# One-hot matrices of two edge stages written by GpSimd, one 128x128 comparison behind each gather, in place of VectorE

## The reference, cut to what matters

```
k_e = k[src] + e ; v_e = v[src] + e            # e = edge_attr @ We
alpha = einsum('ehd,ehd->eh', q[dst], k_e) / sqrt(16)
... softmax over the edges of a destination, then
out = segment_sum(attn * v_e, dst)
```

```
gates = softmax(gate_in @ W_gate + b_gate)      # 3 gates for each edge
out = gates[:,0]*x_src + gates[:,1]*x_dst + gates[:,2]*x_edge
return segment_sum(out, col)
```

## Time and profile before

| | us |
|---|---|
| median of 3 runs | 7088.67 (7060.04 to 7090.18) |
| span of the profiled execution | 7080.9 |
| keys-and-values stage, the gathers' stretch | 1444.0 |
| gate stage, the gathers' stretch | 1430.0 |

### The profile page before, as it was taken

The page is one execution under the profiler, slowest core; times in us unless marked ns, Lnnn a source line. Parts: engine busy times, 40 slices in busy tenths (PEclk is TensorE's granted clock), DMA queues, the critical chain, the costliest instruction groups (busy, mean ns, idle before and its releaser), DMA issues.

```text
span 7080.9 us, 98147 instructions
## 1 busy us (share of the span) xinstructions
PE 4162.5 (59%) x25513; PEld 3308.9 (47%) x25514; DVE 2977.6 (42%) x8318; ACT 1295.5 (18%) x3253; POOL 2894.8 (41%) x2784
## 2 busy tenths in 40 slices
PE   1112000599898455555563664798899666666664
PEld 1001000366565455555553563465565666556654
DVE  3438201411313344444446677212312555555556
ACT  0001000000100211111111664200200322322222
POOL 6778777000000265555553565000000255555555
PEclk6555555799899777777776996899999755655555
DMA  9713000366463455555552451464364222222222
GB/s 361 267 61 135 6 0 0 103 198 192 141 195 118 111 160 158 154 150 156 155 162 89 125 148 30 137 197 138 131 196 145 64 78 78 78 78 79 79 78 69
DMA packets 447985, 885.48 MB, mean 125 GB/s; under 512 B 91722, under 2 KB 278572, under 8 KB 441502
## 3 DMA queue, kind: packets, MB, share of 16 engines
q1 hardware_dynamic: 333406, 608.36, 27.1%
q0 software_dynamic: 106912, 224.30, 11.9%
q10 hardware_dynamic: 7584, 51.91, 2.0%
HBM read 728.93 MB, written 155.35 MB: 125 GB/s over the span
## 4 chain that ended last, share of the span: by engine, by line
PE 33%; DVE 20%; issue 19%; another core or an unknown queue 15%; DVEq 6%; DMA 2%; ACT 2%; ACTq 1%; SPq 0%; POOL 0%; POOLq 0%
PE ps L836 23%; DVE work L1603 3%; PE ps L992 2%; DVE work L624 2%; PE ps L415 1%; DVE work L368 1%; DMA hw<-d_keys 1%; DVE work L1202 1%; DVEq L342 1%; PE ps L1184 1%; DVE hw L438 1%; PE ps L843 1%; PE ps L1182 1%; DMA work<-attr_dram 1%
## 5 line engine op out<-in xcount | busy, mean ns | idle before, releaser
L361 POOL DMA_INDIRECT work<-tab_kv,src_col x832 | 814.1, 978 | 1758.7 <-DMA tab_kv<-hw 1142.1
L361 POOL DMA_INDIRECT work<-tab_gate,src_col x832 | 795.5, 956 | 1795.5 <-DMA tab_gate<-logits 1183.3
L484 POOL DMA_INDIRECT d_adj<-logits,address x782 | 848.1, 1085 | 276.6 <-issue 238.8
L836 PE MATMUL ps<-hw 128*128 128x384 bf16 x5096 | 863.4, 330 | 50.4 <-DVE hw L815 37.1
L836 PE MATMUL ps<-hw,work 128*128 128x384 bf16 x5096 | 845.1, 326 | 0.0
L415 PE MATMUL ps<-work 128*128 128x136 f32 (+1 forms) x3328 | 655.0, 360 | 131.6 <-DVE acc L438 86.4
L836 PEld LDWEIGHTS ps<-hw 128*128 128x128 bf16 x5096 | 502.1, 99 | 383.1 <-issue 53.7
L415 PEld LDWEIGHTS ps<-work 128*128 128x128 f32 x3328 | 599.8, 265 | 165.4 <-issue 165.4
L875 DVE TENSOR_TENSOR work<-work,ps 128x128 f32 (+1 forms) x208 | 59.9, 288 | 1410.0 <-ACT work L867 1409.2
L836 PEld LDWEIGHTS ps<-hw,work 128*128 128x128 bf16 x5096 | 498.8, 98 | 317.7
L1168 PE MATMUL ps<-ident,work 128*128 128x128 f32 x832 | 177.1, 350 | 656.8 <-ACT work L1158 285.2
(11 more groups left out here) (389 smaller groups left out, 6581.4 us busy)
## 6 DMA issues: line engine op xcount, KB each, us to landing
hw<-d_adj SPq DMA_DIRECT2D x104, 800.0 KB, 4.3
work<-d_adj SPq DMA_DIRECT2D x104, 800.0 KB, 4.4
d_adj<-acc SPq DMA_DIRECT2D x52, 1568.0 KB
hw<-d_adj SPq DMA_DIRECT2D x104, 768.0 KB, 4.2
work<-d_adj SPq DMA_DIRECT2D x104, 768.0 KB, 4.3
work<-attr_dram SPq DMA_DIRECT2D x832, 64.0 KB
d_value<-work SPq DMA_DIRECT2D x208, 256.0 KB
work<-d_value SPq DMA_DIRECT2D x208, 256.0 KB, 2.7
```

The source lines that it names most:

```text
L361: pool.indirect_dma_start(rows[:, r * U + u, 0:width], None, table, bass.IndirectOffsetOnAxis(sources[:, at:at + 1], 0)).then_inc(rows_in[ ...
L484: pool.indirect_dma_start(d_adj, bass.IndirectOffsetOnAxis(address[:, tile:tile + 1], 0), counts[:, tile:tile + 1], None).then_inc(adj_out ...
L836: last = nc.tensor.matmul(at, adj_half[2 * s + hf][:, k, :], xs[:, b, :], start=b == 0, stop=b == BLOCKS - 1)
```

## The change: where the one-hot matrices are written

Behind each gather GpSimd now writes the one-hot matrix of the same step itself: a comparison of 128x128 with the step's column of `rel_col` as the operand for each partition. Only the last comparison of a part adds to `hot_ready`. Before the first comparison of a part, and behind the part's first gather, GpSimd waits that the place of the matrices is free: on `att_turned` of part n - 4 in the keys-and-values stage, on `win_done` of part n - 4 in the gate stage. VectorE's two `step_hot` stages go; the one in the stage of the attention sums, which lies between the two, stays.

```diff
-        def gathers(pool, k, table, width, sources, free):
+        def gathers(pool, k, table, width, sources, free, hot_free):
             for n in range(GATHER_TURNS[k] * PARTS):
...
                 for u in range(U):
                     at = n * U + u
                     pool.indirect_dma_start(rows[:, r * U + u, 0:width], None, table,
                                             bass.IndirectOffsetOnAxis(sources[:, at:at + 1], 0)).then_inc(rows_in[r], 16)
+                    if u == 0 and n >= PARTS:
+                        hot_free(n - PARTS)
+                    ins = pool.tensor_scalar(hot[:, r * U + u, :], iota[:], rel_col[:, at:at + 1], None, ALU.is_equal)
+                ins.then_inc(sem("hot_ready"), 1)
...
-            gathers(pool, ATT_PASS, tab_kv, KV, src_col, lambda n: pool.wait_ge(sem("kv_done"), n + 1))
+            gathers(pool, ATT_PASS, tab_kv, KV, src_col, lambda n: pool.wait_ge(sem("kv_done"), n + 1),
+                    lambda n: pool.wait_ge(sem("att_turned"), n + 1))
...
-            edge_loop(dve, [(0, step_hot()), (2, scores)])
+            edge_loop(dve, [(2, scores)])
...
-            gathers(pool, GATE_PASS, tab_gate, GATE_ROW, src_col, lambda n: pool.wait_ge(sem("gate_msg"), n + 1))
+            gathers(pool, GATE_PASS, tab_gate, GATE_ROW, src_col, lambda n: pool.wait_ge(sem("gate_msg"), n + 1),
+                    lambda n: pool.wait_ge(sem("win_done"), gate_sums.done0 + U * (n + 1)))
...
-            edge_loop(dve, [(2, logits), (3, message), (2, gates), (0, step_hot(hot_free)), (4, gate_sums.step_add(dve))])
+            edge_loop(dve, [(2, logits), (3, message), (2, gates), (4, gate_sums.step_add(dve))])
```

More of the change, by code:

```diff
@@ L362, in gathers, with step_hot @@
                                             bass.IndirectOffsetOnAxis(sources[:, at:at + 1], 0)).then_inc(rows_in[r], 16)
-        def step_hot(free=lambda i, r: None):
+                    if u == 0 and n >= PARTS:
+                        hot_free(n - PARTS)
+                    ins = pool.tensor_scalar(hot[:, r * U + u, :], iota[:], rel_col[:, at:at + 1], None, ALU.is_equal)
+                ins.then_inc(sem("hot_ready"), 1)
+        def step_hot():
             def step(i, r):
-                free(i, r)
                 nc.vector.tensor_tensor(hot[:, r * U:(r + 1) * U, :], iota[:].unsqueeze(1).broadcast_to((P, U, P)),
@@ L1608, in gate_dve @@
             dve.wait_ge(sem("gate_zeroed"), 2 * GROUPS + 2)
-            def hot_free(i, r):
-                if not isinstance(i, int) or i:
-                    dve.wait_ge(sem("win_done"), gate_sums.done0 + U * ((i - 1) * PARTS + r + 1))
             chain.after(nc.vector.memset(msg_gate[:, :, GATE_W - 1:GATE_W], 0.0))
             gate_sums.start(dve)
-            edge_loop(dve, [(2, logits), (3, message), (2, gates), (0, step_hot(hot_free)), (4, gate_sums.step_add(dve))])
+            edge_loop(dve, [(2, logits), (3, message), (2, gates), (4, gate_sums.step_add(dve))])
             gate_sums.end(dve)
```

## The result

The changed kernel takes 7817.6 us (median of 4, 7753.8 to 7844.4) beside 7089.4 us (7060.0 to 7124.4) for the kernel before: ratio 1.100, 95% interval 1.095 to 1.106. The prediction said 7402 us with a range up to 7700. The direction was right, the size was not: +728 us where +313 was forecast.

What follows compares the result with a forecast made beforehand. A cycle of waits among GpSimd, VectorE and TensorE, with no engine full, was taken to set the pace; 0 + 267 + 46 = +313 us on the 7080.9 us span gave 7394, as median 7402 us, range 7060 to 7700.

Steps and rivals of the forecast that it cites:

- The step that failed: Both stages: each GpSimd comparison adds 0.29 us to the 1.25 us gather pitch, 1.54 us together.
- the half of the idle time: Keys-and-values stage: half of GpSimd's 390 us idle goes, 241 - 195 = +46 us.
- The ring: Gate stage: a part's first comparison waits for TensorE's sums of part p - 4; 8.11 us a part, +267 us.
- Three links: Gate stage: matrices ready to transposes 0.05 us, transposes and sums 2.88, signal to GpSimd 0.27.
- the fourth: Gate stage: GpSimd's first comparison, then three gathers at 1.25 and three comparisons at 0.29, 4.91 us.
- the lower bound of the prediction: Keys-and-values stage: GpSimd alone sets the pace, 6.16 us a part, 1281 us against 1430, -149 us.
- The comparison is dear: Rival, both stages: a comparison brings its own gap, 0.59 us; gate +450, other +491 less 195; 7840 us, 12%.
- Hidden in the gap: Rival, both stages: the comparison fits the gap behind a gather; gate +90, other -97, 7080 us, 9%.
- The late signals as the cause of the new wait: Gate stage, rival reading: TensorE's signals come about 2 us after the first gather's end, at 3.3 us; changes nothing.
- VectorE's removed 286 us: Both stages: 208 comparisons of 694 ns and 208 of 681 leave VectorE; taken as 0 gain.
- A rule against the change: Gate stage: VectorE's two-input SBUF instruction and GpSimd's comparison lock each other out; some 20 us.

Runs made afterwards that it cites:

- first condition: Jobs, not a change: those where the kernel before takes about 7085 us, as it did for the prediction.
- second condition: Jobs, not a change: those where the same unchanged kernel before takes about 5915 us.
- the first job: The first set of follow-up runs, beside the unchanged kernel before at 7084.4 us.

## Why the prediction was wrong
**The step that failed** is the price of the comparison: "I take 0.29 on top of the pitch, the row nearest in form: gather and comparison together 1.54 us." It measured 0.63 us, and the pitch 1.87. The row nearest in form, L1411, was a product of two tensors. With 128x128 products in the comparisons' place the pitch was 1.58, near the forecast's 1.54, and the gate stage came out as forecast: 1708 us, 8.2 a part, where 8.11 was said. That is partly luck: a product takes 0.41 us and not the 0.29 of a quarter of L1411, but the gap behind it is 0.16 us in place of 0.30. The comparison is dearer than the product by 0.22 us, in pitch by 0.29. The other row behind the 0.29, the selection L1788 with 294 ns in the earlier trace rows, also takes less than half of the comparison's time; the trace of before had no row that would have shown the price.

**A second step failed**, the half of the idle time in the keys-and-values stage. The run with products, where the price was near the forecast's, shows it alone: the stage took 1344 us, 94 less than the 1438 of before, where +46 was forecast.

**The gate stage.** The ring was forecast as 0.05 + 2.88 + 0.27 + 4.91 = 8.11 us and measured 0.06 + 2.87 + 0.10 + 6.21 = 9.24. Three links are right within 0.2 us, the fourth is the mis-sized price: 4 x (0.63 - 0.29) = 1.36, and the measured block is 1.30 longer. The forecast's +267 us became +536: the ring's 1.13 us more, 204 times, are 231 of the difference. The other some 40 us are there because the part shown is a short one: 1951 / 208 = 9.38 us. GpSimd is busy for 1403.5 us in the stage, and 832 x (1.03 + 0.63) are 1381, so its instructions were longer now and then than in that part.

**The keys-and-values stage.** The forecast +46 came as +151. It rested on half of the idle time going, at the price of 0.29. In truth nearly all of it went (390 to 37.7 us), and the price was double: 4 x 1.87 = 7.48 us a part is the lower bound of the prediction with the measured price in it, 1556 us, and the stage took 1589. The two errors partly cancel: with the right price and half the idle time gone, it would have been 4 x 0.62 x 208 - 195 = +321.

**Ahead of the stages** the changed kernel lost 61 us in the first condition, where nothing in it is changed. In the second condition that stretch is the same in both kernels (1840 and 1838). In the first the keys-and-values stage began at 2370 and 2363.5 us in the two kernels without comparisons on GpSimd, and at 2404, 2408, 2427.7 and 2431 in the four with them, with one profile of each (the kernel with half the columns is one of the four); the remote wait at VectorE's `acc` line (L610, L613, L615 or L617) is 90.5 and 172.0 us in the former and 406.3 to 514.9 in the latter. So it may be a cost of the change where signals are late, by a way that the traces don't show, or chance. The 13 runs of the kernel before in the first job lie within 51 us of each other, which speaks against chance alone. The forecast had nothing for it.

**The rivals.** "The comparison is dear" (7840 us, 12%) was nearest in time, with 0.59 for each comparison, but by luck: it is made up of +450 and +296 us, and measured were +536, +151 and the 61 ahead of the stages. Its reason, a gap of the comparison's own, is wrong: there is no gap (0.04 us from a gather's end to the comparison), the instruction itself is long. "Hidden in the gap" holds for a write of 0.12 us and not for a comparison. The late signals as the cause of the new wait fell: GpSimd goes on 0.10 us after the sums' end.

**VectorE's removed 286 us** counted nothing, as forecast: its busy time fell by 229 in the whole run, and neither stage that lost its comparisons became shorter. Of the difference of 57 us, 25 are instructions that are longer now: L1608 takes 358 ns where L1603 took 342, 13 us over 832, and L1590 and L1600 together take 12 us more. The other 32 are time in which a removed comparison overlapped its neighbours, which the page counts once.

**A rule against the change, weighed again.** The comparisons of the changed kernel and VectorE's products of the message, minimum, median and maximum in ns, first and last start:

```profile
L365 POOL TENSOR_SCALAR work<-iota,rels x1664: 610/627/897, 2432.3 to 7759.0; 128x128 f32<-128x128 f32 x185
L1608 DVE SCALAR_TENSOR_TENSOR work<-work x832: 336/340/602, 5834.3 to 7768.5; 128x128 f32<-128x128 f32 x167
```

The trace shows that the two delay each other. In the gate stage 206 of the 832 comparisons overlap an L1608 in time; they take 680 ns on the mean, the other 626 take 623, and all 28 above 0.68 us are among the 206. Of the 832 products 492 overlap a comparison and take 369 ns, the other 340 take 341. That is 12 + 14 = 26 us of work, not all of it on the path. With the comparisons behind the part's gathers, where 824 of the products meet one, those take 417 ns. The Trainium skill (SBUF — State Buffer, "SBUF: two separate sides") speaks of a lock held for the whole instruction; by it I had estimated some 20 us, one comparison in six. The order of the cost agrees (one in four met), the whole-instruction part is not seen: the longest product took 602 ns, and 172 of them lie within a comparison of 610 ns and more, at 423 ns on the mean.

**What stays open.** What makes TensorE's signals late in the first condition, and why they are on time in the stages of the changed kernel there. The runs say: the mere presence of an instruction behind each gather (the 0.12 us write) does not make them go; with comparisons of 0.47 us and more they are gone, placed among the gathers or behind them. A slower pace alone is not it: with half the columns the keys-and-values stage took 1443 us from its first gather to its last, against 1431 in the kernel before, and had no remote wait. But in each of those stages VectorE's own comparison was gone too. Whether GpSimd's comparisons or VectorE's shorter queue take the late signals away is not shown: no run in the first condition had one without the other. That it is TensorE's signals that are late is itself a reading of rows: the waits end up to several us after TensorE's rows, with no instruction ending just then. What in the second condition takes them away altogether is not in the traces.

## What to carry to other kernels
Price an added instruction by a row of the same operation in the same form, not by one of the same shape or by a share of a larger one. If the trace has none, let the forecast be as wide as that doubt (here 0.29 or 0.63 us for the same 128x128), times the number of instructions on the bounding engine, or time the instruction first. Before moving work to the engine that issues the gathers, ask for its busy time together with its issue gaps: it had some 1030 us of 1430 in each stage and was the bound as soon as nothing else held it up. And a wait put between gathers holds up all gathers behind it: the same four comparisons behind a part's gathers cost 405 us less in the gate stage.

## What was not expected of the hardware
- The same kernel takes 7085 us in some jobs and 5915 in others, each within 1%. The difference is in the stretches where gathers run and TensorE's signals are waited for (2370 against 1838, 1438 against 1118, 1415 against 1109), not in the stretch between (1799 against 1791). A ratio depends on it: the same change is 1.100 in the one and 1.223 in the other.
- On GpSimd a 128x128 float32 comparison takes 0.54 (constant) to 0.63 us (an operand for each partition), a product 0.41, 64 columns of the comparison 0.47, a write of 128x832 bytes 0.81.
- Behind a gather there is a gap of 0.30 us in which 0.12 us of other work is free. Behind other work the gap is 0.16 to 0.26. After a comparison the gather is 1.03 us long in place of 0.95, also in the run where only one gather of a part follows a comparison: that one takes 1.03, the other three 0.95.
